# Both chunks of every fourth row in one lot: GpSimd clamps, VectorE takes a maximum and adds in place

## What is computed

```python
s1 = jnp.einsum('bkf,ef->bke', x, W1)        # W = adj, E = 256 values e
s2 = jnp.einsum('bkf,ef->bke', x, W2)
pre = s1[:, :, None, :] + s2[:, None, :, :] + b_lin
h = jnp.where(pre >= 0, pre, 0.2 * pre)
e = jnp.einsum('bije,e->bij', h, a) + bias
attn = jax.nn.softmax(e, axis=2)
out = jax.nn.sigmoid(jnp.einsum('bij,bjf->bif', attn, x))
```

## Time and profile before

| | |
|---|---|
| median of 3 runs | 5788.99 us |
| profiled execution, its time | 5805.18 us |
| profiled execution, span of the trace | 5803.3 us |
| TensorE (PE) busy | 5645.7 us, 97% |
| ScalarE (ACT) busy | 5268.6 us, 91% |
| GpSimd (POOL) busy | 4982.9 us, 86% |
| VectorE (DVE) busy | 4974.7 us, 86% |

### The profile page before, as it was taken

How to read it: one execution, slowest core, us unless ns; L and a number is a source line. 1 busy time by engine, 2 the same in 40 slices (tenths; PEclk the granted TensorE clock), 3 DMA queues, 4 the chain that set the end, 5 groups by cost and what they waited for, 6 DMA issues and landing times.

```text
span 5803.3 us, 127250 instructions
## 1 busy us (share of the span) xinstructions
PE 5645.7 (97%) x40844; PEld 2229.1 (38%) x40844; DVE 4974.7 (86%) x9389; ACT 5268.6 (91%) x12857; POOL 4982.9 (86%) x10246
## 2 busy tenths in 40 slices
PE   8999999999999999999999999999999999999997
PEld 2333333333334333333333333333433333333334
DVE  8888988888888888888898888888888888888883
ACT  8999999999999999999998999999999999999993
POOL 8988988889888888888898888988888888889880
PEclk9999999999999999999999999999999999999999
...
GB/s 14 5 3 7 7 8 4 6 7 7 8 6 3 7 7 8 6 3 7 7 7 8 2 7 7 7 8 6 3 7 7 8 6 3 7 7 7 7 5 6
DMA packets 44539, 37.19 MB, mean 6 GB/s; under 512 B 4736, under 2 KB 39552, under 8 KB 43648
## 3 DMA queue, kind: packets, MB, share of 16 engines
...
...
## 4 chain that ended last, share of the span: by engine, by line
PE 83%; ACT 9%; issue 3%; DVE 3%; POOL 2%; DMA 0%; SPq 0%; POOLq 0%; DVEq 0%; ACTq 0%
PE S L995 52%; PE R L943 13%; ACT ring L798 6%; PE W L943 5%; PE S L943 4%; PE R L1132 2%; PE PA L943 2%; POOL ring L491 1%; PE R L1140 1%; DVE ring L601 1%; PE PB L943 1%; ACT h L840 1%; PE S L987 1%; PE PB L1020 1%; ACT prob L822 0%
## 5 line engine op out<-in xcount | busy, mean ns | idle before, releaser
L491 POOL TENSOR_SCALAR ring<-W,U 128x256 f32<-128x256 f32 x9536 | 4673.8, 509 | 212.8 <-PE S L995 169.3
L798 ACT ACTIVATE ring<-W,U_minus 128x256 f32<-128x256 f32 x10336 | 4239.7, 505 | 0.1
L995 PE MATMUL S<-ring,a_window 128*32 128x512 f32 x32768 | 3732.2, 596 | 52.7 <-DVE ring L601 18.7
L601 DVE TENSOR_TENSOR ring<-U,W 128x512 f32<-128x512 f32 (+1 forms) x3808 | 3187.1, 861 | 3.8 <-PE S L995 3.7
L995 PEld LDWEIGHTS S<-ring,a_window 128*32 128x32 f32 x32768 | 1028.8, 110 | 2464.8 <-issue 2361.9
L596 DVE TENSOR_TENSOR ring<-U,W 128x256 f32<-128x256 f32 x2592 | 1040.4, 407 | 0.0
L462 POOL TENSOR_TENSOR minus_mean<-mv,minus_one 128x4 f32<-128x4 f32 (+1 forms) x160 | 31.5, 197 | 506.8 <-DVE mv L661 469.7
L943 PE MATMUL R<-mT,W 128*128 128x512 f32 (+1 forms) x640 | 332.8, 602 | 2.1 <-ACT mT L902 2.1
L943 PE MATMUL R<-AT,h 128*128 128x256 f32 x1260 | 308.3, 388 | 2.7 <-ACT h L914 2.1
L734 DVE SCALAR_TENSOR_TENSOR rh<-tr,h3T 128x512 f32<-128x512 f32 (+1 forms) x165 | 146.3, 887 | 188.1 <-ACT tr L905 187.8
L738 DVE TENSOR_TENSOR diff<-cand,h3T 128x512 f32<-128x512 f32 (+1 forms) x165 | 192.6, 1167 | 110.3 <-ACT cand L911 110.3
...
## 6 DMA issues: line engine op xcount, KB each, us to landing
...
```

Of the source, the lines that this page charges most:

```text
L491: last = gp.tensor_scalar(ring[:, place, g, half * N:(half + 1) * N], W[:, y, c], LARGEST, U[:, y, c, i:i + 1], ALU.min, ALU.max)
L601: piece = dve.tensor_tensor(ring[:, place, g:g + groups].rearrange("p g (h j) -> p g h j", h=NB), u.unsqueeze(3).to_broadcast([P, groups, ...
L798: last = act.activation(ring[:, place, g, half * N:(half + 1) * N], W[:, y, c], ACT.Relu, bias=U_minus[:, y, c, i:i + 1])
L995: last = pe.matmul(S[y][g * ROWS:(g + 1) * ROWS, :], a_window[:, c, ROWS - 1 - row:2 * ROWS - 1 - row], ring[:, place, g], start=False, st ...
```

## The change

**Summed rows.** Rows 1, 5, 9, ... 29 of each batch (every fourth) become one lot in place of two, so a turn has 112 lots and not 128. TensorE's weights become signs only: the size of `a` is moved into `adj` (`AT_scaled`, `a_abs`), and where the two chunks of a partition have different signs, the block of chunk 1 is taken negative (`sigma`). GpSimd makes the 8 blocks of chunk 1 for the row as a clamp (`signed_blocks`: min with `U_ceiling`, max with `U_floor`, of `W_signed`), and VectorE adds chunk 0 to each in place: `scalar_tensor_tensor(block, w, U, block, max, add)`, where `w` is in PSUM and `block` in the ring. VectorE waits on `signed_ready` ahead of every two such blocks. ScalarE has no part in these lots.

**Other rows.** In the lot of chunk 0 only VectorE and GpSimd make blocks, in the lot of chunk 1 only ScalarE and GpSimd. ScalarE now reads its chunk from PSUM. For that, each batch has two banks, one for each chunk (`W_bank[y][c]`), with U's values in the other half, and the former side banks PA and PB are gone (`side`).

**Shares.** The new `share_blocks` gives these numbers for one turn: VectorE 406 blocks, of them 128 summed ones, each an instruction; the other 278 are 14 instructions of one block, 18 of two, 14 of four, 18 of six and 8 of eight. GpSimd has 153 blocks and 128 signed clamps, ScalarE 337 blocks. In the rows after the layer norms, the shares (VectorE, GpSimd, ScalarE) of the pairs of lots are: lots 40 and 41 (6, 2, 0), (0, 0, 8); lot 42 summed; lots 62 and 63 (8, 0, 0), (0, 7, 1); lots 64 and 65 (8, 0, 0), (0, 0, 8); lot 66 summed; lots 104 and 105 (6, 2, 0), (0, 0, 8); lot 106 summed.

**Around them.** VectorE's `U_minus` goes away. ScalarE's step `evacuate` has seven instructions in place of three. GpSimd computes `U_floor` and `U_ceiling` (128x64 each) at the lot of chunk 1 of row 0. The setup has some small instructions more.

```diff
 RING = 8
-ROUNDS = LOTS // RING
+SUMMED_EVERY, SUMMED_AT = 4, 1
+def summed(t):
+    return t % LOTS_B // EC % SUMMED_EVERY == SUMMED_AT
+def has_lot(t):
+    return not (summed(t) and t % EC)
+LOT_NUMBER = [sum(has_lot(n) for n in range(t)) for t in range(LOTS + 1)]
+ROUNDS = LOT_NUMBER[LOTS] // RING
+SUMMED_LOTS = LOTS // EC // SUMMED_EVERY
...
-VECTOR_BLOCK, VECTOR_START, SCALAR_BLOCK, POOL_BLOCK = 2.67, 0.69, 3.57, 4.5
+VECTOR_BLOCK, VECTOR_START, VECTOR_SUMMED, SCALAR_BLOCK, POOL_BLOCK, POOL_START = 2.67, 0.69, 3.94, 3.57, 4.5, 2.2
 LARGEST = 3.4028234e38
...
-        put(scalar, PRE[h], half, norm=5, copy=2.6, evacuate=12)
+        put(vector, PRE[h], half, stats=5.5)
+        put(scalar, PRE[h], half, norm=7.7, copy=3.6, evacuate=24)
         put(pool, PRE[h], half, stats=20)
...
     shares, v, s, q = [], 0.0, 0.0, 0.0
-    for t in range(LOTS):
-        def ends(share):
-            d, g, a = share
-            return sorted((v + VECTOR_START * (1 + d % 2) + d * VECTOR_BLOCK, q + g * POOL_BLOCK, s + a * SCALAR_BLOCK), reverse=True)
-        d, g, a = min(((d, BLOCKS - d - a, a) for d in range(1, BLOCKS) for a in range(1, BLOCKS - d)), key=ends)
-        shares.append((d, g, a))
-        v += VECTOR_START * (1 + d % 2) + d * VECTOR_BLOCK + vector[t]
-        q += g * POOL_BLOCK + pool[t]
-        s += a * SCALAR_BLOCK + scalar[t]
+    for t in range(0, LOTS, EC):
+        if t % (EC * SUMMED_EVERY) == 0:
+            v += BLOCKS * VECTOR_SUMMED
+            q += BLOCKS * POOL_BLOCK + POOL_START
+        if summed(t):
+            shares += [(BLOCKS, 0, 0), (0, 0, 0)]
+            v += sum(vector[t:t + EC])
+            q += sum(pool[t:t + EC])
+            s += sum(scalar[t:t + EC])
+            continue
+        def costs(d, a):
+            by_pool = [BLOCKS - d, BLOCKS - a]
+            return (v + VECTOR_START * (1 + d % 2) + d * VECTOR_BLOCK,
+                    q + sum(g * POOL_BLOCK + (POOL_START if g else 0) for g in by_pool), s + a * SCALAR_BLOCK)
+        d, a = min(((d, a) for d in range(1, BLOCKS + 1) for a in range(1, BLOCKS + 1)), key=lambda da: sorted(costs(*da), reverse=True))
+        v, q, s = costs(d, a)
+        shares += [(d, BLOCKS - d, 0), (0, BLOCKS - a, a)]
+        v += sum(vector[t:t + EC])
+        q += sum(pool[t:t + EC])
+        s += sum(scalar[t:t + EC])
     return shares
 SHARES = share_blocks()
+VECTOR, POOL, SCALAR = range(3)
+def lots_by(engine, t):
+    place = ring_place(t)[0]
+    having = [n for n in range(LOTS) if has_lot(n) and ring_place(n)[0] == place and SHARES[n][engine]]
+    return sum(n < t for n in having), len(having)
...
         S = [bank("S0"), bank("S1")]
-        W_bank = [bank("W0"), bank("W1")]
-        PA, PB = bank("PA"), bank("PB")
+        W_bank = [[bank(f"W{y}{c}") for c in range(EC)] for y in range(2)]
...
+            def signed_blocks(turn, t):
+                y, p = divmod(t, LOTS_B)
+                place, rnd = ring_place(t)
+                if p // EC == SUMMED_AT:
+                    gp.wait_ge(clamps_ready, turn.at(2, y + 1))
+                need(gp, freed[place], turn.at(ROUNDS, rnd))
+                gp.sem_inc(pool_begun, 1)
+                for g in range(GROUPS):
+                    for half in range(NB):
+                        k = node(t, g * NB + half) // SUMMED_EVERY
+                        last = gp.tensor_scalar(ring[:, place, g, half * N:(half + 1) * N], W_signed[:, y], U_ceiling[:, y, k:k + 1],
+                                                U_floor[:, y, k:k + 1], ALU.min, ALU.max)
+                    last.then_inc(signed_ready, 1)
...
                 d, count, _ = SHARES[t]
-                if p == 0:
-                    gp.wait_ge(u_ready, turn.at(2, y + 1))
-                    gp.wait_ge(w_ready, turn.at(2, y + 1))
+                if row == 0:
+                    gp.wait_ge(uw_ready[c], turn.at(2, y + 1))
+                    if c == 1:
+                        gp.sem_inc(pool_begun, 1)
+                        gp.tensor_scalar(U_floor[:, y], U_signed[:, y], sigma_limit[:], None, ALU.min)
+                        gp.tensor_scalar(U_ceiling[:, y], U_signed[:, y], sigma_limit[:], None, ALU.max).then_inc(clamps_ready, 1)
+                if summed(t):
+                    if c == 0:
...
+                need(dve, freed[place], turn.at(ROUNDS, rnd))
                 if t % LOTS_B == 0:
-                    dve.wait_ge(w_ready, turn.at(2, t // LOTS_B + 1))
+                    dve.wait_ge(uw_ready[0], turn.at(2, t // LOTS_B + 1))
                 while lot["done"] < at_once:
                     one_piece()
...
                 first, end = lot["pieces"][lot["done"]]
                 g, half = group_half(first)
-                w = W_bank[y][:, c * N:(c + 1) * N]
-                if end - first == 1:
+                w = W_bank[y][c][:, 0:N]
+                if summed(t):
+                    if half == 0:
+                        order = sum(summed(n) for n in range(0, t, EC))
+                        dve.wait_ge(signed_ready, lot["turn"].at(GROUPS * SUMMED_LOTS, GROUPS * order + g + 1))
+                    i = node(t, first)
+                    block = ring[:, place, g, half * N:(half + 1) * N]
+                    piece = dve.scalar_tensor_tensor(block, w, U[:, y, c, i:i + 1], block, ALU.max, ALU.add)
+                elif end - first == 1:
                     i = node(t, first)
                     piece = dve.tensor_tensor(ring[:, place, g, half * N:(half + 1) * N],
                                               U[:, y, c, i:i + 1].to_broadcast([P, N]), w, ALU.max)
...
                     piece.then_inc(by_dve[place], 1)
-            def finish_lot():
-                while lot["done"] < len(lot["pieces"]):
+            def finish_lot(t):
...
                     last.then_inc(pre_mv, 1)
-                if p == PRE[1 - y]["evacuate"]:
-                    dve.wait_ge(u_ready, value)
-                    dve.tensor_scalar(U_minus[:, y], U[:, y], -1.0, None, ALU.mult).then_inc(u_minus_ready, 1)
...
             def body(turn):
                 for t in range(LOTS):
                     y, p = divmod(t, LOTS_B)
-                    if turn.has_main:
+                    if turn.has_main and t % EC == 0:
                         start_lot(turn, t)
...
                 row, c = divmod(p, EC)
-                place, rnd = t % RING, t // RING
+                place, rnd = ring_place(t)
+                if c == 0 or summed(t):
+                    return
                 need(act, freed[place], turn.at(ROUNDS, rnd))
-                if p == 0:
-                    act.wait_ge(u_minus_ready, turn.at(2, y + 1))
-                    act.wait_ge(w_ready, turn.at(2, y + 1))
+                if p == EC - 1:
+                    act.wait_ge(uw_ready[1], turn.at(2, y + 1))
                 for n in range(BLOCKS - SHARES[t][2], BLOCKS):
                     g, half = group_half(n)
                     i = node(t, n)
-                    last = act.activation(ring[:, place, g, half * N:(half + 1) * N], W[:, y, c], ACT.Relu,
-                                          bias=U_minus[:, y, c, i:i + 1])
+                    last = act.activation(ring[:, place, g, half * N:(half + 1) * N], W_bank[y][1][:, 0:N], ACT.Relu,
+                                          bias=U_minus[:, y, i:i + 1])
                 last.then_inc(by_act[place], 1)
...
                     act.wait_ge(uw_psum, value)
-                    for c in range(EC):
-                        last = act.activation(U[:, y, c], PB[:, c * N:(c + 1) * N], ACT.Identity, bias=b0_col[:, c:c + 1])
-                    last.then_inc(u_ready, 1)
-                    act.activation(W[:, y], W_bank[y][:].rearrange("p (c n) -> p c n", c=EC), ACT.Copy).then_inc(w_ready, 1)
+                    for c, bank_ in enumerate(W_bank[y]):
+                        act.activation(U[:, y, c], bank_[:, N:2 * N], ACT.Identity, bias=b0_scaled[:, c:c + 1])
+                        if c == 1:
+                            act.activation(U_minus[:, y], bank_[:, N:2 * N], ACT.Identity, bias=minus_b0[:, c:c + 1], scale=-1.0)
+                            act.activation(U_signed[:, y], bank_[:, N + SUMMED_AT:2 * N:SUMMED_EVERY], ACT.Identity, bias=sigma_b0[:], scale=sigma[:])
+                            act.activation(W_signed[:, y], bank_[:, 0:N], ACT.Identity, scale=sigma[:])
+                        act.activation(W[:, y, c], bank_[:, 0:N], ACT.Copy).then_inc(uw_ready[c], 1)
             def post(p, y, value):
                 if p == POST[1 - y]["exp"]:
...
+                place, rnd = ring_place(t)
+                if not has_lot(t):
+                    return
...
-                pe.wait_ge(by_dve[place], turn.at(ROUNDS, rnd + 1))
-                pe.wait_ge(by_act[place], turn.at(ROUNDS, rnd + 1))
-                pe.wait_ge(by_pool[place], turn.at(ROUNDS, rnd + 1))
+                for engine, done in ((VECTOR, by_dve), (POOL, by_pool), (SCALAR, by_act)):
```

(10 more changed lines are left out.)

131 lines of the change are left out of this document (85 added, 46 removed).

## The result

The changed kernel takes 6219.1 us (median of four runs, 6215.5 to 6223.2) against 5789.4 for the kernel before on the same chip: ratio 1.0735 (95% interval 1.0715 to 1.0756). It is 7.4% slower, where I had forecast 2% faster. The profiled execution took 6218.7 us.

The account below looks back on a forecast made before the run. TensorE bounds the kernel now; afterwards VectorE's 162.7 us of work, 9.9 of waits and 1.5 idle make a 174.1 us turn, 4.3 less. Thirty turns give -129, the start +5.5: 5789 - 123.5, rounded 5666 us; range 5440 to 5815.

Parts of the forecast that it names:

- the last term of the sum: Steady turn: idle time left to VectorE as the bound, taken as 1.5 us, between 0 and 2.8.
- the sum: Steady turn: VectorE's work 162.7, waits for GpSimd 9.9 and idle time 1.5 make 174.1 us, 4.3 less than before.
- the tie: Summed rows: VectorE must wait for GpSimd's clamps within a lot, priced at 9.9 us a turn.
- VectorE's work: VectorE's busy time in a steady turn, forecast to rise by 7.5 us from 155.2 to 162.7 us.
- The row of the second turn: Profile before, second turn: ScalarE busy for 148.3 of 151.1 us, taken as the best measure of a bounding engine's idle time.
- The new wait: VectorE waiting for GpSimd's clamps, mainly behind layer norms at lots 42, 66 and 106: 9.9 us a turn.
- The clamp: GpSimd's clamp with two columns, taken at the same step as its ordinary block, 0.452 us.
- Summed block: VectorE's add in place from PSUM and SBUF: a step of 0.39 us, 128 of them 50.3 us a turn.
- rival 3: Slower because a summed block on VectorE takes 0.507 us: 340 us more, 6130 us; chance 0.14.
- Rival 1: TensorE stays the bound, VectorE's waits being hidden: a turn 13 to 14 us shorter, 5390 us; chance 0.25.
- rival 2: No change, within 17 us (0.3%), since the margin of a turn is only 4.3 us; chance 0.07.
- Rival 4: Slower because VectorE's summed blocks hold up GpSimd: up to 50 us more a turn, some 6430 us; chance 0.04.

Follow-up runs that it names:

- e1: Changed kernel with GpSimd's clamps sent to an unread buffer and VectorE adding zeros without waiting for them: 5840.6 us, against 5802.1 for the kernel before.
- e13: e1 with GpSimd making only four of the eight clamps of a summed row: 5781.8 us, against 5787.2 for the kernel before.
- e15: e1 with every fourth of ScalarE's blocks in the other rows one element wide: 5707.0 us, against 5787.2 for the kernel before.
- e3: Changed kernel without summed rows, keeping the split by chunks and banks: 6092.7 us, against 5802.1 for the kernel before.
- e17: e3 with VectorE's and ScalarE's blocks spread over both slots of a row: 5804.4 us, against 5799.0 for the kernel before.
- e18: Changed kernel with clamps issued two lots ahead and blocks spread over both slots of a row: 6044.6 us, ratio 1.0420.
- e11: Changed kernel with ordinary lots shared by three engines and VectorE adding zeros without waiting for clamps: 5925.1 us, against 5805.3 for the kernel before.
- e2: Changed kernel with a constant in place of the column U_ceiling in GpSimd's clamp: 6098.5 us, against 5802.1 for the kernel before.
- e7: Changed kernel with every eighth row summed and all other lots shared by three engines: 5875.9 us, ratio 1.0120.

## Why the prediction was wrong

**The failed step is the last term of the sum: "1.5 us (half of ScalarE's idle time in the second turn, the best row for an engine that is the bound)", beside "the engines ... can bring the fullest of them to 98%, even with two others at 96%".** Without the tie the sum gives 162.7 + 1.5 = 164.2 us; e1 shows 179.0 with VectorE at 161.9 and TensorE at 165.2. The idle time left was 14 us for the fullest engine and 17 for VectorE, not 1.5 (half of the 2.8 in the row is 1.4, which changes nothing). With the tie at 12.0 for 9.9 and VectorE's work at 161.9 for 162.7, that is the whole miss of a steady turn: 15.6 + 2.1 - 0.8 = 16.9 us. The row of the second turn was no measure, for two reasons that e1 shows. In its second turn the fullest engine, GpSimd, is idle for 156.1 - 150.0 = 6.1 us, where the row before has 2.8: the new division and order cost in that same turn. And its steady turn, with more steps in it, has 13.8.

Why those 14 us are idle is open. Lightening one engine gives back 5 at most (e13 to e15), in part through the clock. The order of blocks and steps is one candidate: in the kernel without summed rows it costs 9.1 us, all recovered (e3, e17). Against it stands that spreading gave nothing in e18, that `rh` doesn't wait longer than before, and that e11, with the old division and no tie, still has 9 to 10 us over its fullest engine. That leaves the summed rows themselves, where VectorE finishes a whole lot alone, or the even load of all four engines; no run parts these. What the falling clock adds by itself was not tested apart from the waits that it follows.

**The new wait** was right in place and kind. At lot 42 VectorE waited 2.61 us (forecast 2.3), around lot 66 3.26 (3.9); 13.8 in all for 9.9, and 12.0 by e1. With the slower pace behind it, the wait comes to 10.2 us at lots 42, 66 and 106 (9.4), and to 3.6 at the other summed rows, where I had 0.5. The clamp took 0.533 us, where I took 0.452, and floor and ceiling 0.45 each, where I took 0.35 for both. That lot 66 came so near is luck: GpSimd was slower there than I thought, but VectorE was late too, since it had waited 1.97 us for ScalarE's copy of the bank at 1199.09; without that it would have stood for some 5.2 us, by my estimate.

**The works.** Summed block 0.393 us (0.39): rival 3 fell. ScalarE's blocks follow each other in 0.36 us as forecast (eight from 1205.74 take 3.21 us); its total is 160.7 (158.9), VectorE's 164.8 (162.7). GpSimd's 161.1 for 149.5 is the clamp (128 x 0.081 = 10.4 us) and its small instructions. It is worth 3.4 us a turn by e2, a third of its size. TensorE was 168.7 for 161.5: a granted clock of 0.97 is 2 x 0.03 x 191 = 11 us of the turn at the low level, and up to half of that is lost, 5.7 us (an estimate); the rest of the 7.2 us I can't place.

**The other rivals.** Rival 1 (TensorE stays the bound at 165) failed with the same step as the forecast, by more; rival 2 (no change) is far off. Rival 4 fell as a mechanism: beside summed blocks GpSimd's own take what they took before (1.39 us for three), and its clamps take what they take with VectorE idle. So the case that came, slower, had 0.18, and neither mechanism that I gave it; what came, idle time of all engines together, was not among the rivals.

**By turns.** 30 steady turns x (191.0 - 174.1) = 507 us, and 13.8 and 14.4 us in the first two (159.9 for 146.1, 169.4 for 155.0), make 535 of the 553 us by which the result is above 5666. Against the kernel before, the first two turns lose 14.4 and 18.3 us and a steady one 12.5: the change costs more in the first two turns, where TensorE has less to do.

**Was there a better version?** None that computes the whole result beat the kernel before: e17 comes to 1.0009 by one run, but sums no rows, and e7 to 1.012. What stays open is what else the summed rows cost.
